# Gate products of an mLSTM cross-attention layer: four column groups in another bank, parts added by VectorE, two unary steps on ScalarE

## What is computed

```python
gate_in = jnp.concatenate([q, k, v], axis=-1)
ig = gate_in @ igate_w.T + igate_b
fg = gate_in @ fgate_w.T + fgate_b
...
log_f = jax.nn.log_sigmoid(fg)
csum = jnp.cumsum(log_f, axis=-1)
...
log_D = log_fg_matrix + ig[:, :, None, :]
max_log_D = jnp.max(log_D, axis=-1, keepdims=True)
D = jnp.exp(log_D - max_log_D)
...
C = (qk + k_hop) * D
normalizer = jnp.maximum(jnp.abs(jnp.sum(C, axis=-1, keepdims=True)), jnp.exp(-max_log_D))
h = (C / (normalizer + EPS)) @ vh
```

## Time and profile before

| | |
|---|---|
| median of 3 runs | 3451.86 us |
| the three runs | 3441.05, 3455.0, 3451.86 us |
| span of the profiled execution | 3448.0 us |
| busy in the span: TensorE, VectorE, ScalarE, GpSimd | 88%, 72%, 56%, 59% |

### The profile page before, as it was taken

The page is one execution under the profiler, slowest core; times in us unless marked ns, Lnnn a source line. Parts: engine busy times, 40 slices in busy tenths (PEclk is TensorE's granted clock), DMA queues, the critical chain, the costliest instruction groups (busy, mean ns, idle before and its releaser), DMA issues.

```text
span 3448.0 us, 69897 instructions
## 1 busy us (share of the span) xinstructions
PE 3024.2 (88%) x24660; PEld 1878.3 (54%) x24660; DVE 2480.0 (72%) x5141; ACT 1914.6 (56%) x4581; POOL 2023.7 (59%) x2195
## 2 busy tenths in 40 slices
PE   3777877777778777799999999999999999999997
PEld 2445555454445444455655556556655665566554
DVE  3555555555555555688888888888888888888875
ACT  0444444444444444466666666666666666666663
POOL 3777777777777776255454454554554545545454
PEclk7898888999999999899999999999999999999999
DMA  4999999999999999655555555555555555555542
GB/s 111 322 350 347 326 344 350 341 348 350 347 348 346 347 349 322 190 170 172 172 180 169 162 182 167 172 178 174 174 169 166 182 170 170 178 174 177 171 139 67
DMA packets 412814, 799.46 MB, mean 232 GB/s; under 512 B 107034, under 2 KB 211482, under 8 KB 410420
## 3 DMA queue, kind: packets, MB, share of 16 engines
q1 hardware_dynamic: 311476, 453.08, 42.1%
q0 software_dynamic: 82560, 270.60, 23.5%
q10 hardware_dynamic: 18432, 71.31, 5.3%
HBM read 618.02 MB, written 176.69 MB: 230 GB/s over the span
## 4 chain that ended last, share of the span: by engine, by line
PE 58%; DMA 14%; POOL 11%; issue 6%; DVE 5%; SPq 3%; ACT 3%; POOLq 0%; ACTq 0%; DVEq 0%
DMA arena<-in_L_xattn_rpe_dram,arena 14%; PE psum L1684 11%; PE psum L1605 8%; PE psum L1635 7%; PE psum L1617 7%; POOL arena L749 6%; PE psum L1522 6%; PE psum L1549 5%; PE psum L1538 4%; PE psum L1664 3%; PE psum L1688 3%; PE psum L1580 2%; SPq L585 2%; POOL arena L740 2%; PE psum L1491 1%
## 5 line engine op out<-in xcount | busy, mean ns | idle before, releaser
L749 POOL DMA_INDIRECT arena<-in_L_xattn_rpe_dram,arena x768 | 730.3, 951 | 234.0 <-issue 183.4
L1522 PE MATMUL psum<-arena 128*128 128x128 f32 x4128 | 620.9, 299 | 217.7 <-DMA arena<-in_L_xattn_rpe_dram,arena 203.1
L1522 PEld LDWEIGHTS psum<-arena 128*128 128x128 f32 x4128 | 493.7, 152 | 454.0 <-DMA arena<-in_L_xattn_rpe_dram,arena 317.1
L932 ACT ACTIVATE arena<-arena 128x512 f32<-128x512 f32 (+3 forms) x1024 | 496.8, 555 | 42.8 <-PE psum L1635 39.2
L1684 PE MATMUL psum<-arena 128*128 128x512 f32 x1024 | 494.7, 597 | 3.7 <-DVE arena L1324 1.8
L1274 DVE TENSOR_TENSOR arena<-psum,arena 128x1024 f32<-128x1024 f32 (+1 forms) x384 | 387.1, 1043 | 150.4 <-PE psum L1617 141.1
L543 DVE COPY arena<-psum 128x512 f32<-128x512 f32 x384 | 263.5, 689 | 244.1 <-PE psum L1522 237.9
L552 DVE COPY arena<-psum 128x416 f32<-128x416 f32 (+15 forms) x512 | 225.1, 442 | 288.7 <-PE psum L1538 276.8
L1538 PE MATMUL psum<-arena 64*32 64x416 f32 (+7 forms) x8192 | 368.1, 426 | 59.1 <-ACT arena L854 39.4
L768 POOL TENSOR_SCALAR_AFFINE_SELECT arena<-arena 128x256 f32<-128x256 f32 x256 | 129.0, 504 | 491.2 <-ACT arena L932 490.2
L543 ACT COPY arena<-psum 128x512 f32<-128x512 f32 x384 | 225.8, 588 | 283.6 <-PE psum L1522 279.8
(11 more groups left out here) (110 smaller groups left out, 4725.9 us busy)
## 6 DMA issues: line engine op xcount, KB each, us to landing
arena<-in_x_dram SPq DMA_DIRECT2D x256, 256.0 KB, 4.3
arena<-gate_rows SPq DMA_DIRECT2D x128, 512.0 KB, 4.4
arena<-in_x_dram SPq DMA_DIRECT2D x512, 64.0 KB
arena<-in_ctx_dram SPq DMA_DIRECT2D x32, 1024.0 KB, 7.4
out_dram<-arena SPq DMA_DIRECT2D x128, 256.0 KB, 2.1
arena<-in_L_xattn_rpe_dram,arena POOLq DMA_INDIRECT x1032
arena<-hop_products SPq DMA_DIRECT2D x128, 128.0 KB, 2.6
arena<-hop_products SPq DMA_DIRECT2D x128, 120.0 KB, 2.6
```

Of the source, the lines that this page charges most:

```text
L749: nc.gpsimd.indirect_dma_start(out=rows[set_of(n, v)][:, t, :], out_offset=None, in_=rpe[:, :], in_offset=bass.IndirectOffsetOnAxis(ap=her ...
L932: last = nc.scalar.activation(decay[u % DECAYS][:, e, at:at + width], top_pair[p % 2][:, e * S + j * P:e * S + j * P + width], ACT.Exp, bi ...
L1522: last = nc.tensor.transpose(turn_bank(o)[:, q * P:(q + 1) * P], own[:, q * P:(q + 1) * P], ident)
```

## The change

- `gates` writes to bank 4 (`GATE_BANK`). Part k of the contraction goes to partitions 32k to 32k+31 (`GW` = 32), first the queries' part, then the context's, accumulated in place. So there are still 8 products of 512 columns, now on four 32-column groups of the array instead of two wider ones; each group holds a quarter of the contraction, of both gates. Forget gate rows are 0 to 7 of a group, input gate rows 8 to 15.
- The four quarters are added: ScalarE copies groups 2 and 3 to `g_ctx`, VectorE adds three times (`two`, in PSUM, `half`, `zi`), 32x512 each.
- `abs` and `min` leave VectorE; ScalarE makes |z| and relu(-z). `logf` goes: the running sum adds ln(.) and relu(-z) itself, with the other sign, and the two later steps turn their sign accordingly.
- Input gate rows lie in partitions 8 to 15 and are needed in 0 to 7: SyncE moves them by a DMA of 8 rows (`move_igate`), between the loads of the next queries and context; `gates_3` waits for it.
- TensorE waits for the sum of pair 0 ahead of the gates, since both use bank 4; on VectorE that sum stands ahead of value means 1 and 2. `base(rf, 0)` no longer waits for `zi`; `weigh(6)`, first into bank 4 after it, does.
- In the setup the gates' weights and biases are laid out and turned for the new rows.

```diff
@@ -119,6 +119,7 @@
     BODIES = SEG_GROUPS // QUARTERS
     FG = 32
     GR = FG + NH
+    GW = P // KT
 
 
     Q_OFF = {3: 0, 0: 512, 2: 640, 1: 1024}
...
@@ -384,6 +387,7 @@
         C_TURN, C_BANK = [0, 0, 1, 1], [4, 7, 6, 7]
         X_TURN, X_BANK = [1, 1, 2, 2], [6, 7, 6, 6]
         MIX_AT = 2 * P
+        GATE_BANK = 4
 
         BACK = {2: 0, 3: 1, 5: 2}
         def pair_bank(p):
@@ -393,11 +397,11 @@
                       [(n, t) for t in (2, 3) for n in ("stats", "mean")] +
                       [("norm", 2), ("vsum", 0), ("vmean", 0), ("norm", 3)] +
                       [(n, t) for t in (1, 2, 3) for n in ("vsum", "vmean")] +
-                      ["zi", "abs", "min", "logf", "cum", "a", "cmax", "maxlog"])
+                      ["two", "half", "zi", "cum", "a", "cmax", "maxlog"])
         pe_p = Stage(sem("pe_p"), [("c", t) for t in tiles] + [("x", t) for t in tiles] + ["gates", "stats"])
         act_p = Stage(sem("act_p"), [(n, t) for t in (0, 1) for n in ("ln", "rstd")] +
                       [("c", 0), ("c", 1), ("ln", 2), ("rstd", 2), ("c", 2), ("c", 3), ("x", 0), ("x", 1),
-                       ("ln", 3), ("rstd", 3), ("x", 2), ("x", 3), "gctx", "exp", "ln", "floor", "stats"])
+                       ("ln", 3), ("rstd", 3), ("x", 2), ("x", 3), "gctx", "abs", "relu", "exp", "ln", "floor", "stats"])
         pool_p = Stage(sem("pool_p"), [("center", t) for t in tiles])
 
         hop_loaded = [sem(f"hop_loaded{i}") for i in range(2)]
...
@@ -642,6 +646,11 @@
                 sp.wait_ge(*dve_f.at(r.b, ("x1", (t - 2) % ST), 1 if t < 2 else 0))
                 sp.dma_start(x_res[t % 2], x_tiles[r.b, t, :, :]).then_inc(xr_loaded[t % 2], 16)
 
+            def move_igate(r):
+
+                sp.wait_ge(dve_p.sem, dve_p.done(r.b, "zi"))
+                sp.dma_start(g_i, g_zi[NH:2 * NH, :]).then_inc(igate_moved, 16)
+
             def store_out(r, t):
                 tile = r.b * ST + t
                 sp.wait_ge(*dve_f.at(r.b, ("out", t)))
@@ -679,6 +688,9 @@
                     load_residual(rf, 3)
                 if rn:
                     load_queries(rn)
+                if rp:
+                    move_igate(rp)
+                if rn:
                     load_context(rn)
                 if rf:
                     store_out(rf, 0)
@@ -991,11 +1003,16 @@
                 def gate_context():
                     act.wait_ge(pe_p.sem, pe_p.done(rp.b, "gates"))
                     act.wait_ge(dve_p.sem, dve_p.done(rp.b, "a", 1))
-                    nc.scalar.copy(g_ctx[0:GR, :], bank(6)[2 * FG:2 * FG + GR, :]).then_inc(
+                    nc.scalar.copy(g_ctx[0:2 * GW, :], bank(GATE_BANK)[2 * GW:4 * GW, :]).then_inc(
                         act_p.sem, act_p.step("gctx"))
 
                 def gate_log():
-                    act.wait_ge(dve_p.sem, dve_p.done(rp.b, "abs"))
+                    act.wait_ge(dve_p.sem, dve_p.done(rp.b, "zi"))
+                    nc.scalar.activation(g_l[0:NH, :], g_zi[0:NH, :], ACT.Abs).then_inc(
+                        act_p.sem, act_p.step("abs"))
+                    nc.scalar.activation(g_m[0:NH, :], g_zi[0:NH, :], ACT.Relu, scale=-1.0).then_inc(
+                        act_p.sem, act_p.step("relu"))
+                    act.wait_ge(act_p.sem, act_p.done(rp.b, "abs"))
                     nc.scalar.activation(g_l[0:NH, :], g_l[0:NH, :], ACT.Exp, scale=-1.0).then_inc(
                         act_p.sem, act_p.step("exp"))
                     act.wait_ge(act_p.sem, act_p.done(rp.b, "exp"))
...
@@ -1231,28 +1248,28 @@
 
                 def gates_1():
                     dve.wait_ge(act_p.sem, act_p.done(rp.b, "gctx"))
-                    nc.vector.scalar_tensor_tensor(g_zi[0:GR, :], bank(6)[0:GR, :], g_b[0:GR, :], g_ctx[0:GR, :],
-                                                   ALU.add, ALU.add).then_inc(dve_p.sem, dve_p.step("zi"))
-                    dve.wait_ge(dve_p.sem, dve_p.done(rp.b, "zi"))
-                    nc.vector.scalar_tensor_tensor(g_l[0:NH, :], g_zi[FG:GR, :], -1.0, g_zi[FG:GR, :], ALU.mult,
-                                                   ALU.max).then_inc(dve_p.sem, dve_p.step("abs"))
-                    nc.vector.tensor_scalar(g_m[0:NH, :], g_zi[FG:GR, :], 0.0, None, ALU.min).then_inc(
-                        dve_p.sem, dve_p.step("min"))
+                    got = bank(GATE_BANK)
+                    nc.vector.tensor_tensor(got[GW:2 * GW, :], got[GW:2 * GW, :], g_ctx[GW:2 * GW, :],
+                                            ALU.add).then_inc(dve_p.sem, dve_p.step("two"))
+                    if rp.b:
+                        dve.wait_ge(igate_moved, rp.b * 16)
+                    nc.vector.scalar_tensor_tensor(g_zi[0:GW, :], got[0:GW, :], g_b[0:GW, :], g_ctx[0:GW, :],
+                                                   ALU.add, ALU.add).then_inc(dve_p.sem, dve_p.step("half"))
+                    dve.wait_ge(dve_p.sem, dve_p.done(rp.b, "half"))
+                    nc.vector.tensor_tensor(g_zi[0:GW, :], g_zi[0:GW, :], got[GW:2 * GW, :],
+                                            ALU.add).then_inc(dve_p.sem, dve_p.step("zi"))
 
                 def gates_2():
                     dve.wait_ge(act_p.sem, act_p.done(rp.b, "ln"))
-                    dve.wait_ge(dve_p.sem, dve_p.done(rp.b, "min"))
-                    nc.vector.tensor_tensor(g_m[0:NH, :], g_m[0:NH, :], g_l[0:NH, :], ALU.subtract).then_inc(
-                        dve_p.sem, dve_p.step("logf"))
-                    dve.wait_ge(dve_p.sem, dve_p.done(rp.b, "logf"))
                     dve.wait_ge(act_p.sem, act_p.done(rp.b, "floor", 1))
-                    nc.vector.tensor_tensor_scan(g_c[0:NH, :], one[0:NH, :].to_broadcast([NH, S]), g_m[0:NH, :], 0.0, ALU.mult,
+                    nc.vector.tensor_tensor_scan(g_c[0:NH, :], g_l[0:NH, :], g_m[0:NH, :], 0.0, ALU.add,
                                                  ALU.add).then_inc(dve_p.sem, dve_p.step("cum"))
 
                 def gates_3():
                     dve.wait_ge(dve_p.sem, dve_p.done(rp.b, "cum"))
                     dve.wait_ge(pe_p.sem, pe_p.done(rp.b, "stats", 1))
-                    nc.vector.tensor_tensor(g_rows[0:NH, :], g_zi[0:NH, :], g_c[0:NH, :], ALU.subtract).then_inc(
+                    dve.wait_ge(igate_moved, rp.b * 16 + 16)
+                    nc.vector.tensor_tensor(g_rows[0:NH, :], g_i, g_c[0:NH, :], ALU.add).then_inc(
                         dve_p.sem, dve_p.step("a"))
                     dve.wait_ge(dve_p.sem, dve_p.done(rp.b, "a"))
 
@@ -1261,7 +1278,7 @@
                     nc.vector.tensor_tensor_scan(g_z[0:NH, :], g_rows[0:NH, :], g_rows[0:NH, :], -3.0e38, ALU.max,
                                                  ALU.max).then_inc(dve_p.sem, dve_p.step("cmax"))
                     dve.wait_ge(dve_p.sem, dve_p.done(rp.b, "cmax"))
-                    nc.vector.tensor_tensor(g_c[0:NH, :], g_c[0:NH, :], g_z[0:NH, :], ALU.add).then_inc(
+                    nc.vector.tensor_tensor(g_c[0:NH, :], g_z[0:NH, :], g_c[0:NH, :], ALU.subtract).then_inc(
                         dve_p.sem, dve_p.step("maxlog"))
 
                 def unit_weights(u):
@@ -1414,11 +1431,11 @@
 
                 if ra:
                     two_weights(2)
+                if ra:
+                    pair_sums(ra, 0)
                 if rp:
                     value_means(1)
                     value_means(2)
-                if ra:
-                    pair_sums(ra, 0)
                 if rf:
                     layer(rf, 1)
                 if rp:
@@ -1575,10 +1592,12 @@
 
 
                     pe.wait_ge(act_p.sem, act_p.done(rp.b, ("x", ST - 1)))
-                    for k in range(KT):
-                        for lo, w, src in ((0, gate_qT, qT[rp.par]), (2 * FG, gate_cT, kT[rp.par])):
-                            last = nc.tensor.matmul(bank(6)[lo:lo + GR, :], w[:, k, :], src[:, k, :],
-                                                    start=(k == 0), stop=(k == KT - 1))
+                    if ra:
+                        pe.wait_ge(dve_o.sem, dve_o.done(ra.b, ("sum", 0)))
+                    for i, (w, src) in enumerate(((gate_qT, qT[rp.par]), (gate_cT, kT[rp.par]))):
+                        for k in range(KT):
+                            last = nc.tensor.matmul(bank(GATE_BANK)[k * GW:(k + 1) * GW, :], w[:, k, :],
+                                                    src[:, k, :], start=(i == 0), stop=(i == 1))
                     last.then_inc(pe_p.sem, pe_p.step("gates"))
 
                 def gate_stats():
@@ -1629,6 +1648,9 @@
                             pe.wait_ge(act_p.sem, act_p.done(rp.b, ("c", 0)))
                     if k == 0:
                         pe.wait_ge(dve_o.sem, dve_o.done(ra.b, ("sum", (p - 2) % 4), 1 if p < 2 else 0))
+                        if p == 2 and rp:
+                            pe.wait_ge(act_p.sem, act_p.done(rp.b, "gctx"))
+                            pe.wait_ge(dve_p.sem, dve_p.done(rp.b, "zi"))
```

(3 more changed lines are left out.)

18 lines of the change are left out of this document (10 added, 8 removed).

## The result

| | before | after |
|---|---|---|
| median, same chip | 3453.43 us | 3555.74 us |
| the runs | 3441.05 to 3458.53 (4) | 3554.52 to 3560.53 (4) |
| span of the profiled execution | 3448.0 us | 3558.8 us |
| mean period of the full rounds | 62.82 us | 66.54 us |
| ratio, 95% interval | | 1.0305, 1.0283 to 1.0327 |

The change makes the kernel slower by 102 us in the medians, and by 110.8 us in the spans of the two profiled executions. The periods account for the latter: 30 x (66.54 - 62.82) = 112 us. So all of it lies in the rounds.

The account below looks back on a forecast made before the run. TensorE, busy 62.11 of 62.82 us a round, was taken as the bound. Chain +1.96 and clock +1.0 over 30 rounds add 89 us to the 3448.0 span, 3537; the forecast was 3538 us, range 3466 to 3580.

Parts of the forecast that it names:

- (a): TensorE's rounds: the chain is late but the clock holds, 30 x 1.96 = +59, 3510 us; chance 0.25.
- (b): VectorE is not held by GpSimd: +0.4 us a round, +12, 3464 us; chance 0.10 with its neighbours.
- (c): TensorE does not wait for ScalarE, so 1.72 us a round is gained: -52, 3400 us; chance 0.07.
- (d): VectorE held everywhere and the clock falls too: 30 x (3.5 + 1.7) = +156, 3604 us; chance 0.08.
- The four groups overlap in full: Gate products on TensorE: four at a time take 1.82 us instead of 3.54, gain 1.72 us a round.
- Sum 0 is in time: VectorE's sum 0, started after ScalarE's square, ends 0.3 us before the gate products start; no cost.
- VectorE's chain: VectorE from the sums through router and gates: `zi` ends at 2625.15, 2.1 us later than before.
- ScalarE: `abs` and `relu` ahead of `exp` take 1.05 us with the handoff; mixT ends at 2627.77.
- The chain on TensorE: Last base product (L1688), 1.47 us after mixT, starts at 2629.24 instead of 2627.28: +1.96 us a round.
- The idle time: TensorE stands some 3.3 us in each round before the transpose that waits for mixT.
- The clock: TensorE's granted clock falls after the idle time: between 0 and 1.7 us a round, taken as 1.0.
- What was taken as free: SyncE's input gate move, GpSimd's later centrings ahead of the masks, and VectorE's dropped `logf`: no cost or gain.

Follow-up runs that it names:

- gates_x3: The kernel after with the gate products issued three times over: 3508.66 us, ratio 1.0173 to the kernel before.
- before_half: The kernel before with half of the gate products left out, so its output is another: 3449.0 us, ratio 0.9997.
- sums_last: The kernel after with VectorE's old order, sums of pair 0 behind value means 1 and 2: 3509.46 us, ratio 1.0174 to the kernel before.

## Why the prediction came out right

The forecast of 3538 us, slower, lies 18 us under the measured 3555.74, inside the range of 3466 to 3580; the rivals (a) at 3510, (b) at 3464, (c) at 3400 and (d) at 3604 all lie further off. Step by step, with times from the start of the gate products in the round shown:

- **The four groups overlap in full.** Forecast 1.82 us, measured 1.86. By the ratio of the Trainium skill (TensorE: Matmul & The Clock Gate, Part 3) it would have been about 2.3, an estimate; with 128 rows in four groups the measurement decides, and it is within 0.04 us of full overlap.
- **Sum 0 is in time.** VectorE idled 2.05 us (forecast 2 us) for the square, and the sum ended 0.42 ahead of the products (forecast 0.3).
- **VectorE's chain.** The four sums and means took 3.13 us (forecast 3.15). The layer's first step was not held, 0.68 as taken. The router came at 4.34 (forecast 4.75), `zi` ended at 9.73 (9.90). A part of this nearness is luck: from the layer's first step to the router it took 2.31 us where I had 2.6, and from the router to the gates 3.21 (2684.70 to 2687.91) where I had 2.95, and the two misses cancel.
- **ScalarE.** `abs` and `relu` cost 1.06 ahead of `exp` (forecast 1.05). mixT ended at 12.39 (12.52).
- **The chain on TensorE.** At full clock the last base product (L1688's successor, L1710 there) starts at 13.98 (gates_x3, 2661.54 less 2647.56), against 12.03 before: +1.95, forecast +1.96. Of it 1.75 arrived in the period; the 0.2 that later waits give back I had named and left out.
- **The idle time.** Forecast 3.3 us, measured 3.66. The router was 0.4 earlier than I had it, so base 0 started at 6.02 instead of 6.55 and left a longer stand.
- **The clock: the term that was mis-sized.** I took +1.0 a round, from 3.4 us at half clock, less a part inside the idle time and less some spared rounds. It measured +1.97 between the profiled executions, 1.57 between the medians. No round was spared, and in every second one the clock stayed low about twice as long as in the earlier trace rows, which put even my upper bound of 1.7 too low for those rounds (2.5). By the Trainium skill (TensorE: Matmul & The Clock Gate, Part 1) the throttled clock is the default, and activity lifts it. For idle times of 3.67 us the counts above agree with it in all rounds, for those of 2.08 and 2.60 in 5 and 14 of 26.
- **What was taken as free** was free: the move of the input gate by SyncE, `logf`, the masks. Among the waits of TensorE and VectorE in the rounds there is none for a DMA or a mask.

The terms measured are 1.75 + 1.97 = 3.72 a round, and 30 x 3.72 = 112 against the 110.8 between the spans. The forecast had 2.96: 0.21 too much for the chain, 0.97 too little for the clock, so the two errors offset each other in part. The profiled execution after was the slowest of its four runs, so against the medians the loss is 102; between the spans, for which the sum was made (3537), the miss is 22 us and not 18.

One step was wrong without showing in the sum: I read the kernel before as bound by TensorE alone, so that "whatever is cut from its instructions, or added to its waits, goes straight into the period". before_half disproves the first half of that. VectorE's `zi`, which bank 6 waits for, was an equal bound, and rival (c) with its -52 us was therefore too simple: with mixT nearly in time the packing alone brings 28.

## What to carry to other kernels

When an edit shortens the work of the engine that bounds a pipelined loop, list the chains that end within a few tenths of it before counting the gain: here two, `zi` for bank 6 and mixT behind `gate_log`. Don't put steps that are moved to another engine into its queue ahead of a copy that the bounding engine waits for; here the same steps behind three more calls turned 3% slower into 0.7% faster, and with two more moves into 1.4%. And an idle time of TensorE in one piece can be paid twice, once as itself and once in the clock: here in all rounds at 3.67 us, in half of them at 2.60, in none at 0.36.

## What was not expected of the hardware

- TensorE lost its clock in a loop where it was busy 94% of the time (62.95 of 67.10 us), in every round. Of the 4.15 us of idle time 3.66 came in one piece; that this, and not the sum, decides was not tested by itself. Issuing the gate products again, 1.72 us of useless work a round, took 44 us off.
- The cost of a fall was not one number. It was 1.64 us in sums_last, and some 1.4 and 2.5 in turn in the kernel after, by how long the clock stayed low and how much of that lay in the idle time.
- The layer's first step on VectorE took 1.41 us in the old order and 0.68 in the new one, with the same operands. It is so in all rounds between 1560 and 3300 us: 1.35 to 1.41 in the kernel before and again in sums_last, 0.68 in the kernel after. When it runs decides its length. That GpSimd's work beside it does this was argued, and no run here took GpSimd's work away; in the kernel after GpSimd was at work beside it as well (L809, 2681.41 to 2683.95), so its being busy is not enough. The three gate steps and sum 0, which read a matmul bank, took 0.68 to 0.74 in the round shown.
